# Second attention of a six-phase network on one core: its head computed in two halves, and smaller fills of the value buffers

## The chip, the cores and the metric

The kernel runs on one core of one Trainium2 chip. The metric is the time of one execution on the device, in microseconds (us). The time before is the median of three runs, 2862.56 us (2862.47 to 2865.04).

The engines are PE (matmuls; PEld is its weight load), DVE (vector), ACT (activation), POOL (GpSimd) and SP, which issues transfers. Each works off its own instructions strictly in order, and waits on semaphores for the others.

## The reference, cut to what matters

The network adds six blocks to `x` of 4 x 1024 tokens by 256: a routed feed-forward, a landmark attention, the feed-forward again, then an expert block, a quaternion attention and the expert block again. The change lies in the fifth. Its computation, for each of four groups of 1024 tokens that the kernel calls batches (in the reference, x of the whole call passes through `_layernorm`, then the attention):

```
z = layernorm(x)                       # mean and variance over 256
q = norm(quat_linear(z, qW, qb))       # four components of 64, divided by
k = norm(quat_linear(z, kW, kb))       # the root of their squares' sum
v = quat_linear(z, vW, vb)
s = q_h . k_h / 4 + constant           # 16 heads of 16
x = x + quat_linear(softmax(s) @ v, oW, ob)
```

## The kernel before, in words

Everything stays in SBUF: `X` holds all tokens as 32 tiles of 128 tokens by 256. The six phases are classes with a list of items each. An item is a tuple such as `("pj", n, b, x, h, cc)`. All five engines walk the same list and each does its own part of an item (methods `pe`, `act`, `dve`, `pool`, `sp`), with waits on semaphores whose values are counted from the list beforehand (`COUNTS`, L2827). So the order of the list is the order on every engine. If an item has a part on DVE that waits for ACT, everything behind it on DVE waits too.

**The phase `Attn1`** (L2819) works on four batches b of 8 tiles. Halves h are 4 tiles, or 512 tokens. `cc` is one of the two halves of the 256 columns; x is 0 for queries and 1 for keys. Batch 0 is prepared ahead of the loop by `start` (L2875); the other three are prepared piece by piece inside the loop of 256 turns (`order`, L2971). A turn is one key tile of one group of four heads: two pairs of score matmuls (`qk`), two exponentials of 128x1024 on ACT (L3262), and four value products (`pv`). What the head does for batch 0, and on which engine:

- `fill` (L170 to L178): matmuls of ones into an unused bank, two passes for each one asked.
- `stats` (DVE, L194, L197): mean and variance of four tiles.
- `root` (DVE, L207 to L218): twelve short instructions, each waiting for the one before, on columns of the eight tiles: the reciprocal root of the variance by a bit trick and three Newton steps. The slice of tiles comes from `rooted` (L3292), which can take a half already.
- `zz` (DVE, L3327, L222): four normalised tiles, into `ZS`. Item `(zz, n, 0, h)` is half h.
- `ht` (PE L3124, ACT L3235, DVE L3346): four transposes into a bank; ACT writes the rounded part `HB`, DVE the rest `HL`.
- `pj` (PE L162 to L164, ACT L3240; for the second query half DVE L3354): a projection of 128 columns for 512 tokens, six matmuls; the copy to `QL` adds the bias.
- `sq` (DVE L3366, L3367, L3369): the product of `QL` with itself for both column halves, and their sum; three instructions with both inputs in SBUF, the third with a wait.
- `nn` (PE L170, eight matmuls; ACT L3252, L3254): sum over the components, then the root's reciprocal by logarithm and exponential.
- `p1`, `p2`, `p3` (DVE L3389, ACT L3307, DVE L3398): `QL` times the norm, its rounded part, the rest.
- `sta` (PE L3112, then ACT L3246 or DVE L3403): these parts are placed into the rows `S` that the score matmuls read.
- `vv` (PE L162 to L164, twelve matmuls; DVE L3379): the values of two tiles, written into the value buffer.
- `put` (SP L3458): parts to a buffer in DRAM, for the later groups of heads.

**The value buffers** `V` are two tensors of 128 x 2192: 8 tiles x 16 heads x 17 columns, and 16 more. Of 17 columns, 16 are values and the last is 1, so that the value product also gives the softmax's denominator. A product reads 32 columns from a head's first one; the last head's read goes 15 beyond the 17th column, into the 16 at the end. `vone` (POOL, L3440) fills both tensors with 1.0 at the start of the phase, before the values are written into them.

**POOL's other part** is `xb` (L3446): the output bias is added to the eight tiles of `X` after both halves of `zz`, eight additions of 128x256 that read and write SBUF.

Around the head: the phase before ends with an item at which all engines meet (L3513). The first item of the head on PE is `fill` of 6, and the last is the first `qk`, which needs the keys of both halves and the queries of the first (L3112). The first batch's other items (`rest`) come in the first turns of the loop.

Of the kernel before, what the change touches and what calls it, by code (L numbers as in the profile page):

```python
# [97 lines left out]
class Chip:  # L98
# [61 lines left out]
    def mm3(self, e, o, lh, ll, rh, rl, start, stop):  # L160

        e.matmul(o, lh, rh, start=start, stop=False, skip_group_check=True)  # L162
        e.matmul(o, ll, rh, start=False, stop=False, skip_group_check=True)  # L163
        return e.matmul(o, lh, rl, start=False, stop=stop, skip_group_check=True)  # L164

    def mm_by_columns(self, e, o, l, r, start, stop):

        for j in range(4):
            js = slice(32 * j, 32 * j + 32)
            ins = e.matmul(o[js, :], l[:, js], r, start=start, stop=stop, skip_group_check=True)  # L170
        return ins
# [68 lines left out]
class Ffn0:  # L240
# [4 lines left out]

    COUNTS = {
        "up": {"up": 2, "sil": 1, "mul": 1}, "lo": {"hi": 1, "lo": 1},
        "down": {"dn": 1}, "yo": {"yo": 4, "yod": 2}, "sca": {"sca": 96}, "zput": {"zo": 16},
        "wt": {"wh": 1, "wo": 1},
        "norm": {"z": 1},  # L250
        "tp": {"ax": 1, "aa": 1, "fh": 1, "al": 1}, "lg": {"ax": 1}, "lv": {"lv": 1}, "lb": {"ax": 1, "ad": 1},
        "best": {"best": 1}, "oh": {"oh": 1}, "tot": {"ax": 1, "ad": 1}, "pos": {"ax": 1, "ad": 1, "gd": 1, "ge": 1},
        "slot": {"pm": 1},
        "oa": {"oa": 1}, "sl": {"sl": 1}, "tab": {"ad": 1, "tab": 1},
# [5 lines left out]
    def __init__(self, chip, call, first):  # L260
# [53 lines left out]
        for it in self.items:  # L314
            counts = dict(self.COUNTS.get(it[0], {}))
            if it[0] == "consts":
# [618 lines left out]
class Attn0:  # L935
# [7 lines left out]

    COUNTS = {
# [92 lines left out]
    def banks(self, p):  # L1037
# [3 lines left out]
        for it in self.items:  # L1041
            counts = dict(self.COUNTS.get(it[0], {}))
            p.count(it, counts)
# [35 lines left out]
    def pe(self, e, w, it):  # L1079
        c, p, n, k = self.c, self.c.p, self.call, it[0]  # L1080
        mm = lambda o, l, r, a=True, z=True: e.matmul(o, l, r, start=a, stop=z, skip_group_check=True)  # L1081
        if not self.COUNTS.get(k, {}).get("pp"):
            return
# [1023 lines left out]
class Ffn1:  # L2107
# [5 lines left out]
    CONSTS1 = 7, 11, 15, 19, 23, 27, 31, 39, 43, 47, 57, 60  # L2113
    COUNTS = {"b1": {"gb": 16}, "b1t": {"b1t": 1, "b1c": 1}, "io": {"io": 2, "b2z": 1}, "mh": {"wh": 1}, "mk": {"wo": 1}, "b2": {"b2l": 32, "b2": 1},
# [704 lines left out]
class Attn1:  # L2819
# [5 lines left out]

    ahead = ()
    PARTS = ((0, 1, 0), (0, 0, 1))  # L2827
    COUNTS = {"root": {"rt": 1}, "vone": {"vone": 2}, "zz": {"zb": 1}, "xb": {"xb": 8},
# [46 lines left out]
    def start(self):  # L2875

        n = self.call
        seq = []
        hts = lambda h: [("ht", n, 0, h, cc) for cc in range(2)]
        parts = lambda x, h: [(k, n, 0, x, 0, h) for k in ("p1", "p2", "p3")]  # L2880
        pj = lambda x, h, cc: ("pj", n, 0, x, h, cc)
        seq.append(("fill", n, 6))
        seq += [("stats", n, "p", 0, 0), ("stats", n, "p", 0, 4), ("root", n, "p", 0), ("zz", n, 0, 0), ("zz", n, 0, 1)]
        seq += hts(0) + hts(1) + [pj(1, 0, 0), pj(1, 0, 1), ("sq", n, 0, 1, 0)]
        seq += [pj(1, 1, 0), pj(1, 1, 1), ("nn", n, 0, 1, 0), ("sq", n, 0, 1, 1), pj(0, 0, 0)] + parts(1, 0)
        seq += [pj(0, 0, 1), ("sq", n, 0, 0, 0), ("nn", n, 0, 1, 1), ("vv", n, 0, 0)] + parts(1, 1)
        seq += [("nn", n, 0, 0, 0)] + [("sta", n, 1, jj, h) for h in range(2) for jj in range(2)] + [("put", n, 1)]
        seq += parts(0, 0) + [("fill", n, 3)] + [("sta", n, 0, jj, 0) for jj in range(2)]
        rest = Jobs()
        rest.add(0, pj(0, 1, 0))  # L2890
        rest.add(1, pj(0, 1, 1), ("sq", n, 0, 0, 1))
        rest.add(1, ("vv", n, 0, 1))
        rest.add(1, ("nn", n, 0, 0, 1), *parts(0, 1))
        rest.add(1, ("vv", n, 0, 2))
        rest.add(1, ("sta", n, 0, 0, 1))
        rest.add(1, ("sta", n, 0, 1, 1), ("put", n, 0), ("stk", n, 1))
        rest.add(1, ("vv", n, 0, 3), ("xb", n, 0))
        for x in range(2):
            for k in ("p1", "p2", "p3"):
                rest.add(1, (k, n, 0, x, 1))  # L2900
        return seq, rest
# [413 lines left out]
    def dve(self, e, w, it):  # L3315
        c, p, n, k = self.c, self.c.p, self.call, it[0]
# [10 lines left out]
        elif k == "zz":  # L3327
            b, h = it[2:]
            if b:
                w.wait_ge(*p.at("pp", ("nn", n, b - 1, 1, 1) if b > 1 else ("nn", n, 0, 0, 1)))  # L3330
            w.wait_ge(*p.at("rt", ("root", n, "p", b)))
            for i in range(4 * h, 4 * h + 4):
                ins = c.normalise(e, self.ZB[:, i, :], 8 * b + i)
            ins.then_inc(*p.one("zb"))
        elif k == "ht":
            b, h, cc = it[2:]
# [11 lines left out]
        elif k == "pj" and self.by(it) == "fv":  # L3348
            b, x, h, cc = it[2:]
# [6 lines left out]
        elif k == "sq":  # L3356
            b, x, h = it[2:]
# [6 lines left out]
            pj = ("pj", n, b, x, h, 1)  # L3364
# [5 lines left out]
        elif k == "vv":  # L3370
            b, i2 = it[2:]
# [11 lines left out]
        elif k == "p1":  # L3383
            b, x, cc = it[2:5]
            h, hs = it[5] if len(it) > 5 else 1, self.span(it)
# [6 lines left out]
        elif k == "p3":  # L3392
            b, x, cc = it[2:5]
# [5 lines left out]
        elif k == "sta" and self.by(it) == "fv":  # L3399
            x, jj, h = it[2:]  # L3400
# [9 lines left out]
        elif k == "ft":  # L3410
            u = it[2]
            b, g, hf = self.half(8 * u)
# [9 lines left out]
        elif k == "fb":  # L3422
            b, h, cc = it[2:]
# [3 lines left out]
        elif k == "fo":  # L3427
            b, i2 = it[2:]
# [6 lines left out]
    def pool(self, e, w, it):  # L3435
        c, p, n, k = self.c, self.c.p, self.call, it[0]
        if k == "vone":
            for v in self.V:
                w.wait_ge(*p.mine())
                e.memset(v[:, :], 1.0).then_inc(*p.one("vone"))  # L3440
        elif k == "xb":
            b = it[2]
            w.wait_ge(*p.at("zb", ("zz", n, b, 1)))
            for i in range(8 * b, 8 * b + 8):
                w.wait_ge(*p.mine())
                e.tensor_tensor(c.X[:, i, :], c.X[:, i, :], self.k.BVO[:, 1, :], ALU.add).then_inc(*p.one("xb"))  # L3446
# [233 lines left out]
```

## Time and profile before

| | |
|---|---|
| median of three runs | 2862.56 us |
| the profiled execution's own time | 2869.36 us |
| its span | 2867.6 us |
| PE busy | 2766.3 us, 96% |
| DVE busy | 1834.8 us, 64% |
| ACT busy | 1633.8 us, 57% |
| POOL busy | 551.3 us, 19% |
| mean granted TensorE clock | 0.990 |

The profile is of one execution. Its times count from the first instruction, and the execution's own time is 1.8 us longer than the span. Busy time is the sum of an engine's instructions. A timeline row gives the start, the duration, the engine, the line of the kernel, what is written from what, and in brackets how long the engine stood idle before it and what it then waited for. The granted clock is a share of 2.4 GHz. Merged rows (x4, x8) give the time from the first start to the last end.

### The profile page before, as it was taken

Reading aid. Unit: us, or ns where it says so; the run is one execution under the profiler, and the core shown is the slowest. Engines: PE = TensorE matmul, PEld = TensorE weight load, DVE = VectorE, ACT = ScalarE, POOL = GpSimd, SP = SyncE. Lnnn points to the kernel's source line nnn. Section 1 sums busy time; section 2 is a strip of 40 time slices with the busy share of each in tenths; the row PEclk is TensorE's granted clock in tenths of the full one; section 3 lists DMA queues with packets and bytes.
Section 4 is the critical chain, followed back from the end, with each engine's and each line's share of the span. In section 5 each row is a group of like instructions: output and inputs, shape, how many; then the busy total and the mean of one; then the engine's idle time right before and its main releaser. Section 6 shows DMA issues by size and latency. Waiting matters only on the chain.

```text
span 2867.6 us, 56389 instructions
## 1 busy us (share of the span) xinstructions
PE 2766.3 (96%) x23301; PEld 2160.6 (75%) x23301; DVE 1834.8 (64%) x3730; ACT 1633.8 (57%) x2473; POOL 551.3 (19%) x479
## 2 busy tenths in 40 slices
PE   9999999998999999999999988998999999998998
PEld 7888999996777778889999965996343434333998
DVE  8775555548887787755555567887545464436786
ACT  4434454543443455344554433776887888892786
POOL 0002224221000000021323146553000000001454
PEclk9999999999999999999999999999999999999999
DMA  5123333332000022233433253774452252513686
GB/s 169 63 67 115 95 88 84 86 92 70 2 3 24 3 71 82 67 98 87 102 77 93 77 160 119 212 212 118 100 133 52 70 116 80 113 38 119 181 215 149
DMA packets 237312, 279.77 MB, mean 98 GB/s; under 512 B 23267, under 2 KB 218496, under 8 KB 237056
## 3 DMA queue, kind: packets, MB, share of 16 engines
q1 hardware_dynamic: 204992, 229.78, 27.3%
q0 software_dynamic: 30720, 45.85, 8.5%
q8 instruction: 184, 3.01, 0.5%
q10 hardware_dynamic: 1344, 0.53, 0.1%
q14 instruction: 72, 0.59, 0.1%
HBM read 204.58 MB, written 72.88 MB: 97 GB/s over the span
## 4 chain that ended last, share of the span: by engine, by line
PE 78%; DVE 11%; ACT 4%; issue 3%; POOL 2%; DMA 1%; POOLq 0%; DVEq 0%; ACTq 0%
PE PS L162 18%; PE PS L164 17%; PE PS L163 17%; PE PS L3112 13%; PE PS L1081 6%; PE PS L170 2%; POOL ZR L222 1%; DVE SM L194 1%; ACT FW L581 1%; DVE SM L1461 1%; ACT Z L626 1%; PE PS L515 1%; DVE FW L666 1%; PE PS L3205 1%; DVE PROD L654 1%
## 5 line engine op out<-in xcount | busy, mean ns | idle before, releaser
L3262 ACT ACTIVATE P<-PS 128x1024 f32<-128x1024 f32 x512 | 484.5, 1045 | 85.3 <-PE PS L3112 83.4
L162 PE MATMUL PS<-FH,FW 128*128 128x366 f32 (+1 forms) x1408 | 504.5, 358 | 9.3 <-ACT SIL L559 4.7
L164 PE MATMUL PS<-FH,FW 128*128 128x366 f32 (+1 forms) x1408 | 497.7, 353 | 0.0
L163 PE MATMUL PS<-FH,FW 128*128 128x366 f32 (+1 forms) x1408 | 496.9, 353 | 0.0
L567 ACT ACTIVATE FHH<-PROD 128x366 fp32r<-128x366 f32 (+1 forms) x352 | 194.3, 552 | 421.3 <-DVE PROD L654 394.3
L162 PE MATMUL PS<-FW,FHH 128*122 128x256 f32 (+1 forms) x1184 | 338.5, 286 | 1.5 <-DVE FHH L661 1.5
L163 PE MATMUL PS<-FW,FHH 128*122 128x256 f32 (+1 forms) x1184 | 332.4, 281 | 0.0
L164 PE MATMUL PS<-FW,FHH 128*122 128x256 f32 (+1 forms) x1184 | 332.0, 280 | 0.0
L654 DVE TENSOR_TENSOR PROD<-SIL,PS 128x366 f32<-128x366 f32 (+1 forms) x352 | 206.6, 587 | 157.6 <-PE PS L164 137.2
L661 DVE TENSOR_TENSOR FHH<-PROD,FHH 128x366 fp32r<-128x366 f32 (+1 forms) x352 | 208.9, 594 | 147.3 <-ACT FHH L567 145.2
L162 PEld LDWEIGHTS PS<-FH,FW 128*128 128x128 f32 x1408 | 265.5, 189 | 35.4 <-ACT SIL L559 8.4
L164 PEld LDWEIGHTS PS<-FH,FW 128*128 128x128 f32 x1408 | 265.2, 188 | 22.5
L163 PEld LDWEIGHTS PS<-FH,FW 128*128 128x128 f32 x1408 | 265.5, 189 | 19.0 <-issue 1.0
L3112 PE MATMUL PS<-P,V 128*32 128x512 f32 x2048 | 273.4, 606 | 1.3 <-DVE OC L3409 0.3
L666 DVE TENSOR_TENSOR FW<-WST,FW 128x1536 fp32r<-128x1536 f32 x96 | 168.7, 1757 | 138.4 <-ACT FW L581 131.4
L559 ACT ACTIVATE SIL<-PS 128x366 f32<-128x366 f32 (+1 forms) x352 | 180.7, 513 | 124.3 <-PE PS L164 119.5
L879 POOL DMA_INDIRECT xa_scratch<-Z,RV x84 | 139.7, 1664 | 533.5 <-ACT Z L626 481.1
L162 PEld LDWEIGHTS PS<-FW,FHH 128*122 128x122 f32 (+1 forms) x1184 | 219.6, 185 | 5.6 <-DVE FHH L661 2.3
L163 PEld LDWEIGHTS PS<-FW,FHH 128*122 128x122 f32 (+1 forms) x1184 | 219.6, 185 | 2.3
L164 PEld LDWEIGHTS PS<-FW,FHH 128*122 128x122 f32 (+1 forms) x1184 | 219.6, 185 | 0.0
L869 POOL DMA_INDIRECT Z<-zn_scratch,RV x84 | 96.0, 1143 | 515.5 <-DVE RV L843 429.0
L3112 PE MATMUL PS<-S,S 64*128 64x512 f32 x1024 | 193.0, 451 | 1.6 <-DVE S L3403 1.0
(485 smaller groups left out, 5557.0 us busy)
## 6 DMA issues: line engine op xcount, KB each, us to landing
WS<-L_ffn_w_dram SPq DMA_DIRECT2D x256, 256.0 KB
WST<-L_ffn_W_dram SPq DMA_DIRECT2D x168, 256.0 KB
S<-parts_scratch SPq DMA_DIRECT2D x60, 384.0 KB, 7.6
parts_scratch<-PT SPq DMA_DIRECT2D x28, 512.0 KB, 3.8
WST<-L_ffn_W1s_dram SPq DMA_DIRECT2D x40, 256.0 KB
WST<-L_ffn_W3s_dram SPq DMA_DIRECT2D x40, 256.0 KB
WST<-L_ffn_W2s_dram SPq DMA_DIRECT2D x40, 256.0 KB
xa_scratch<-X SPq DMA_DIRECT2D x17, 512.0 KB, 5.1
```

The costliest lines, as they stand in the source:

```text
L162: e.matmul(o, lh, rh, start=start, stop=False, skip_group_check=True)
L163: e.matmul(o, ll, rh, start=False, stop=False, skip_group_check=True)
L164: return e.matmul(o, lh, rl, start=False, stop=stop, skip_group_check=True)
L559: e.activation(self.SIL[:, h, 0:NH], c.bank(2 * self.up_at[it] % 3, NH), ACT.Silu).then_inc(*p.one("sil"))
L567: e.activation(self.FHH[:, s % 2, 0, hs], self.PROD[:, h, 0:NH], ACT.Copy).then_inc(*p.one("hi"))
L654: e.tensor_tensor(self.PROD[:, h, 0:NH], self.SIL[:, h, 0:NH], c.bank((2 * self.up_at[it] + 1) % 3, NH), ALU.mult).then_inc(*p.one("mul"))
L661: e.tensor_tensor(self.FHH[:, s % 2, 1, hs], self.PROD[:, h, 0:NH], self.FHH[:, s % 2, 0, hs].bitcast(F32), ALU.subtract).then_inc(*p.one( ...
L666: e.tensor_tensor(self.fw(q)[:, 1, :], self.WST[:, q % 2, :], self.fw(q)[:, 0, :].bitcast(F32), ALU.subtract).then_inc(*p.one("wo"))
L879: e.indirect_dma_start(out=c.XA, out_offset=bass.IndirectOffsetOnAxis(ap=self.TO.bitcast(U32)[:, 6 * e_ + t:6 * e_ + t + 1], axis=0), in_= ...
L1081: mm = lambda o, l, r, a=True, z=True: e.matmul(o, l, r, start=a, stop=z, skip_group_check=True)
L3112: mm = lambda o, l, r, a=True, z=True: e.matmul(o, l, r, start=a, stop=z, skip_group_check=True)
L3262: e.activation(self.PR[K % 3][:, 2 * jj:2 * jj + 2, :].rearrange("p a b -> p (a b)"), c.pair(2 * ((2 * K + jj) % 3)), ACT.Exp, scale=0.25) ...
```

## The change

The list of the head is rewritten for halves. The root is now two items of four tiles, and `zz` of the first half follows its root directly; the statistics of the second half, its root and its rows come later. One `fill` is added, and the order of the projections, squares, norms and parts differs. Each `zz` of batch 0 waits for its own root. POOL fills only every 17th column and the last 16 of each value buffer, in four instructions in place of two.

```diff
-    COUNTS = {"root": {"rt": 1}, "vone": {"vone": 2}, ...
+    COUNTS = {"root": {"rt": 1}, "vone": {"vone": 4}, ...
...
         seq.append(("fill", n, 6))
-        seq += [("stats", n, "p", 0, 0), ("stats", n, "p", 0, 4), ("root", n, "p", 0), ("zz", n, 0, 0), ("zz", n, 0, 1)]
-        seq += hts(0) + hts(1) + [pj(1, 0, 0), pj(1, 0, 1), ("sq", n, 0, 1, 0)]
-        seq += [pj(1, 1, 0), pj(1, 1, 1), ("nn", n, 0, 1, 0), ("sq", n, 0, 1, 1), pj(0, 0, 0)] + parts(1, 0)
-        seq += [pj(0, 0, 1), ("sq", n, 0, 0, 0), ("nn", n, 0, 1, 1), ("vv", n, 0, 0)] + parts(1, 1)
+        seq += [("stats", n, "p", 0, 0), ("root", n, "p", 0, 0), ("zz", n, 0, 0), ("stats", n, "p", 0, 4)]
+        seq += hts(0) + [("fill", n, 1), ("root", n, "p", 0, 1), ("zz", n, 0, 1)]
+        seq += [pj(1, 0, 0), pj(1, 0, 1), ("sq", n, 0, 1, 0)] + hts(1) + [pj(0, 0, 0), ("nn", n, 0, 1, 0), pj(0, 0, 1)]
+        seq += [pj(1, 1, 0), pj(1, 1, 1)] + parts(1, 0)
+        seq += [("sq", n, 0, 1, 1), ("sq", n, 0, 0, 0), ("nn", n, 0, 1, 1), ("vv", n, 0, 0)] + parts(1, 1)
         seq += [("nn", n, 0, 0, 0)] + [("sta", n, 1, jj, h) for h in range(2) for jj in range(2)] + [("put", n, 1)]
...
-            w.wait_ge(*p.at("rt", ("root", n, "p", b)))
+            w.wait_ge(*p.at("rt", ("root", n, "p", b) if b else ("root", n, "p", b, h)))
...
             for v in self.V:
                 w.wait_ge(*p.mine())
-                e.memset(v[:, :], 1.0).then_inc(*p.one("vone"))
+                e.memset(v[:, 16:2176:17], 1.0).then_inc(*p.one("vone"))
+                w.wait_ge(*p.mine())
+                e.memset(v[:, 2176:2192], 1.0).then_inc(*p.one("vone"))
```

## Rows read from the trace of the kernel before

**Rows 1.** The page, part 4: the chain that ended last, by engine.
```profile
PE 78%; DVE 11%; ACT 4%; issue 3%; POOL 2%; DMA 1%; POOLq 0%; DVEq 0%; ACTq 0%
```

**Rows 2.** Timeline of PE: start, us, line, out<-in, idle before and releaser.
```profile
1250.72 0.79 PE L162 MATMUL PS<-FH,FW 128*128 128x512 f32 x1 [2.78 <-issue]
...
1973.07 5.42 PE L178 MATMUL PS<-ONES 128*128 128x512 f32 x12 [0.83 <-DVEq L3513]
1982.09 3.67 PE L3124 MATMUL PS<-IDENT,ZS 128*128 128x128 f32 x16 [3.60 <-DVE ZS L222]
...
1988.10 0.40 PE L162 MATMUL PS<-HB,WHk 128*128 128x512 f32 x1
...
1989.47 0.39 PE L162 MATMUL PS<-HB,WHk 128*128 128x512 f32 x1
...
1992.66 1.06 PE L170 MATMUL PS<-ONT,SQM 128*32 128x512 f32 x8 [0.30 <-DVE ONT L3369]
1993.65 0.50 PE L162 MATMUL PS<-HB,WHq 128*128 128x512 f32 x1
...
1997.59 0.39 PE L162 MATMUL PS<-WHv,HB 128*128 128x256 f32 x1
...
2007.62 0.73 PE L3112 MATMUL PS<-S,S 64*128 64x512 f32 x4 [1.04 <-DVE S L3403]
...
2046.91 0.66 PE L3124 MATMUL PS<-IDENT,ZS 128*128 128x128 f32 x4
2047.49 0.73 PE L3112 MATMUL PS<-S,S 64*128 64x512 f32 x4
```

**Rows 3.** Stretches: us, busy PE, PEld, DVE, ACT, POOL (instructions), PEclk, DMA, GB/s.
```profile
1250.00:1254.00 4.00, 3.28 (x9) 2.70 (x10) 0.36 (x1) 0.60 (x1) 1.60 (x2) 0.57 0.75 233
...
1982.00:1985.70 3.70, 3.61 (x17) 3.38 (x17) 2.77 (x8) 1.79 (x3) 2.13 (x3) 0.50 1.09 362
```

**Rows 4.** Timeline of DVE: statistics, first root step and rows of the head.
```profile
1973.10 1.41 DVE L194 BATCH_NORM_STATS2 SM<-X 128x6 f32<-128x256 f32 x4
...
1976.81 1.59 DVE L207 TENSOR_SCALAR SM<-SM 128x8 f32<-128x8 f32 x1
...
1980.65 2.67 DVE L222 TENSOR_SCALAR ZS<-X,SM 128x256 f32<-128x256 f32 x8
```

**Rows 5.** Timeline of DVE: first and last of the next root's twelve instructions.
```profile
2025.71 0.17 DVE L207 TENSOR_SCALAR SM<-SM 128x8 f32<-128x8 f32 x1
...
2027.94 0.17 DVE L218 SCALAR_TENSOR_TENSOR SM<-SM 128x8 f32<-128x8 f32 x1
```

**Rows 6.** Timeline of POOL in the head.
```profile
1972.91 1.55 POOL L2556 DMA_INDIRECT xa_scratch<-YE,SM  x1 [0.30 <-issue]
1973.89 4.49 POOL L3440 MEMSET V<- 128x2192 f32 x2
1983.41 6.40 POOL L3446 TENSOR_TENSOR X<-X,BVO 128x256 f32<-128x256 f32 x8 [5.03 <-DVE ZS L222]
```

**Rows 7.** POOL's groups by form: a short fill; busy us, mean ns, idle before.
```profile
L2744 POOL MEMSET SQM<- 128x128 f32 x1 | 0.2, 204 | 0.1
```

**Rows 8.** Timeline of DVE: the first squares, and a subtraction behind ACT's rounding.
```profile
1990.49 0.69 DVE L3366 TENSOR_TENSOR ONT<-QL 128x512 f32<-128x512 f32 x1 [3.30 <-ACT QL L3240]
...
1996.59 0.69 DVE L3398 TENSOR_TENSOR QLR<-QL,PT 128x512 fp32r<-128x512 f32 x1 [0.72 <-ACT PT L3307]
```

**Rows 9.** Timeline of ACT: a projection's copy, and the rounding of a part.
```profile
1989.67 0.69 ACT L3240 ACTIVATE QL<-PS,C 128x512 f32<-128x512 f32 x1 [0.68 <-PE PS L164]
...
1995.93 0.62 ACT L3307 ACTIVATE PT<-QL 128x512 fp32r<-128x512 f32 x1
```

**Rows 10.** Timeline of all engines near 1753: DVE's products beside POOL's.
```profile
1751.23 2.71 POOL L2770 TENSOR_TENSOR Wk<-WLk,C 64x256 f32<-64x256 f32 x4
...
1753.26 0.21 DVE L2494 TENSOR_TENSOR PX<-PX 128x64 f32<-128x64 f32 x1
1753.51 0.52 DVE L2496 TENSOR_TENSOR PX<-PX 128x64 f32<-128x64 f32 x1
```

More of the change, by code:

```diff
@@ L2827 @@
     PARTS = ((0, 1, 0), (0, 0, 1))
-    COUNTS = {"root": {"rt": 1}, "vone": {"vone": 2}, "zz": {"zb": 1}, "xb": {"xb": 8},
+    COUNTS = {"root": {"rt": 1}, "vone": {"vone": 4}, "zz": {"zb": 1}, "xb": {"xb": 8},
               "ht": {"pp": 1, "fv": 1}, "eb": {"eb": 1}, "sta": {"pp": 1}, "sq": {"sqv": 1}, "p1": {"prv": 1}, "qk": {"qkp": 1, "ex": 1},
```

## The prediction

> **What bounds the kernel now.** I began with the page's chain of waits: 78% of what ended last is PE, 11% DVE, 4% ACT [rows 1]. So time moves where PE stands still, and the diff touches one such place, the head of the second attention. I then read the timelines of the engines from 1973 us, where the expert phase has ended, to the first score matmul at 2007.62 [rows 2]. From there on the list is untouched and PE nearly back to back; so **the change is worth what it does to that 2007.62**, and I expect the shift to reach the end whole.
>
> Inside the head PE isn't the limit. It waits 3.60 us for DVE's rows before the transposes [rows 2], and those run at a granted clock of 0.50, the 1.2 GHz level [rows 3]. DVE first takes the statistics of four tiles twice, 1.86 us each (half of 1973.10 to 1976.81). Then the root's first step takes 1.59 us [rows 4], where the same step of the next root takes 0.17 [rows 5]. It ends at 1978.40; POOL's fills of the value buffers end at 1973.89 + 4.49 = 1978.38 [rows 6]. I read that as DVE shut out by POOL.
>
> **The change, step by step.** It halves the root and the rows, takes the fills nearly away, and reorders the list. I rebuilt the schedule from durations of before; a time below is on that execution's axis.
>
> 1. *Fills.* A fill of 128x128 takes 0.20 us [rows 7]; four fills of 128 or 16 columns with their gaps are under 1 us, but they start only when the indirect transfer leaves POOL (1972.91 + 1.55) [rows 6], so they end near 1975.3. The root now starts at 1974.96. Bounds of its wait: 0 and 0.35 us; I take 0.2. Some 1.2 us of the 1.42 us stall are gone.
> 2. *First half.* A root is twelve steps; without the stall it takes 2.42 us (2025.71 to 2028.1) [rows 5]. The steps are 8 columns wide, so I charge four tiles the same. 1974.96 + 0.2 + 2.42 = 1977.58. Four rows of the eight that take 2.67 are 1.33 [rows 4], and PE is let go 1.44 after they start (1980.65 to 1982.09) [rows 2, 4]: transposes at **1979.02**, 3.07 earlier. At full clock four transposes take 0.58 (2046.91 to 2047.49) [rows 2]: both groups are done at 1980.20, the new fill (two passes of 0.45, where 12 take 5.42) at 1981.10 [rows 2]. DVE is in the second statistics until 1978.91 + 1.86 = 1980.77, then makes two subtractions of a 128x512 tile, 0.69 each at most [rows 8], and PE starts its projections at 1982.25. A projection of six matmuls is 1.37 (1988.10 to 1989.47) [rows 2]: two end at 1984.98.
> 3. *Second half.* The second root is 2.42 us of DVE that was not there: 1982.05 to 1984.47. Rows until 1985.80, transposes 1985.91 to 1987.09, a query projection to 1988.45. ACT copies the second projection 0.2 after its end (1989.47, 1989.67) and DVE squares 0.74 later [rows 2, 9]: 1985.92. Before it was 1990.49 [rows 8], so here the change is 4.57 ahead.
> 4. *A collision that was not there.* POOL's eight additions of the output bias (6.40 in all, 0.73 and a gap each) wait for the second rows. Before, they ran 1983.41 to 1989.81 [rows 6], and DVE's first product with both inputs in SBUF came at 1990.49 [rows 8]. Now they start at 1985.91, on top of the squares. What an overlap costs is seen at 1753: while POOL multiplies out of SBUF, a DVE product of 128x64 takes 0.52 instead of 0.21; the one of 0.21 stands right behind another [rows 10]. The squares are three instructions, the second right behind the first, the third behind a wait of its own: I charge two waits of one POOL addition, 1.45. Bounds 0 and 2.2 (three waits). The squares let PE go 2.17 after their start (1990.49 to 1992.66) [rows 2, 8]: 1985.92 + 2.17 + 1.45 = 1989.54. The norm sum takes 0.99 (1992.66 to 1993.65) [rows 2], then come a query projection and both of the keys' second half, 3 x 1.37: PE is through at **1994.63**. Without the collision at 1993.5.
> 5. *The order behind it.* The list puts the three parts of the keys' first half behind both late key projections and ahead of the late squares. ACT's rounding copy so queues behind ACT's copies of those projections: the last one 1994.83 to 1995.43 (a pass of ACT over 128x512 takes 0.62) [rows 9]. DVE's subtraction comes 0.66 after the rounding starts (1995.93, 1996.59) [rows 8, 9], at 1996.09, and the squares queued behind it at 1996.72. PE's next item is the norm sum of these: 1996.72 + 2.17 = **1998.89; PE stands 4.26 us**.
> 6. *The end of the head.* Norm sum 0.99, then the value projection: 1999.88 against 1997.59 [rows 2], 2.29 late. From there to 2007.62 every step is the same in the same order: **+2.3 us** at full clock.
> 7. *The clock.* Behind PE's idle of 3.60 us the stretch 1982 to 1985.7 has 0.50, behind one of 2.78 (at 1250.72) the stretch 1250 to 1254 has 0.57 [rows 2, 3]. Behind 4.26 I expect it again. Norm sum and value projection then cost up to their length once more, 1.0 and 1.3 (of 0.99 and 1.5): **+2.3**. Bounds 0 and 3.5 (the fill behind them too, if its slack is gone). PE's full clock at the front is in the times above.
>
> SP's transfers keep their places and are late by the same amount; nothing before 2028 waits for one.
>
> **Sum:** +1.2 (the order and the second root, all gains counted), +1.1 (the collision: what PE's slack leaves of 1.45), +2.3 (clock) = +4.6. The profiled execution took 2869.36 (span 2867.6 and 1.8 around it), 6.8 above the median of 2862.56; with the sum it is 2874.0, and on the median **2867.2**. A measurement can tell 0.2%, 5.7 us, from no change; this lies inside.
>
> *A rule weighed.* The rows at 1753 show a neighbour that paid nothing [rows 10]. The Trainium skill, page "SBUF — State Buffer", section "Who interferes with whom", says that a DVE instruction with two SBUF inputs and a GpSimd instruction that reads SBUF exclude each other, the second to issue waiting out the whole first. Taken at its word for each of the three instructions, the squares pay 2.2.
>
> **Rivals.**
> - *One of the two prices is missing.* Collision without the low clock: +2.3, 2864.9. Low clock without collision: +3.6, 2866.2. For it: PE worked for long ahead of the gap. Chance 0.22.
> - *Neither*: +1.2, 2863.8. Chance 0.08.
> - *Three waits in the squares*, POOL slipping in between each two: +0.7 more, 2867.9; against it stands the free neighbour. Chance 0.08. The page's rule would give this.
> - *Slower*: PE's clock falls in the middle too. Between 1981.1 and 1989.5 PE idles 1.15, 0.9 and 1.1 us. If the level is low from about 1987, the projections behind cost up to 1.2 more each (DVE hides a part), and the tail is low again: +6.2, 2868.8. It decides from an idle near 2.8 us, the shortest that has a low stretch behind it in my rows; two more us of delay in the squares would make one. Chance 0.12.
> - *Faster*: PE has its last first-half work done 2 us earlier than before; if the rounding did not hold the late squares, the tail would start early: -1.5, 2861.0. Against it: each engine takes the list strictly in order. Chance 0.10.
> - *It doesn't do what it says*: the strided fills still hold the root, for 1 us: +0.8 on top of any case; inside the range.
>
> **Numbers.** The forecast has 0.40. All cases but the slower one lie in 2861 to 2868; with the unknowns of the clock and a spread of 2.6 us between the runs I take 2860.5 to 2870.5. Slower by over 0.2% (above 2868.3): most of the slower rival and the upper part of the forecast, 0.20. Faster by as much needs -5.7: 0.02. Same: 0.78.
>
> **What would show it.** The first root step under 0.5 us; transposes near 1979; the first squares stretched beside POOL's additions; an idle of PE near 4 us ahead of the norm sum of the keys' second half, with a clock near 0.5 behind; the first score matmul 36.8 to 39.1 us after the first statistics (before: 2007.62 - 1973.10 = 34.52). I am wrong if that distance is under 34.5, if PE has no idle over 2 us there, or if the loop swallows the shift.

## The result, and the profile after

The changed kernel takes 2866.69 us in the median of 21 runs (2863.47 to 2871.78), the kernel before 2862.94 beside it (21 runs, 2860.28 to 2865.25). The ratio is 1.0015, with a 95% interval of 1.0009 to 1.0021: slower by some 4 us. That is inside the 0.2% that I had called "same", on the side and of about the size that was forecast (+4.6).

In one profiled execution of each, the head grows by more than the medians differ. Let D be the time from the first statistics to the first score matmul: 34.52 us before, 2007.63 - 1967.36 = **40.27** after. Everything after it keeps its length in this pair: from the first score matmul to the end of the span 859.98 us before, 859.37 after. Over the fourteen profiled executions shown below that stretch lies between 855.9 and 860.0, and for the kernel before it is 3.5 shorter in its second profile than in its first. So a total follows D only loosely; here the interval of the ratio, +2.6 to +6.0 us, holds both the 3.75 of the medians and the 5.75 of D. (The head starts at 1967.36 here and at 1973.10 before; over the executions shown below this start moved between 1967.4 and 1977.8, and the change can't reach what lies ahead of it. So times below are compared from the first statistics on.)

The timeline of DVE of the changed kernel; the first rows answer to [rows 4], the squares to [rows 8]:

```profile
1967.36 1.41 DVE L194 BATCH_NORM_STATS2 SM<-X 128x6 f32<-128x256 f32 x4
...
1969.21 0.36 DVE L207 TENSOR_SCALAR SM<-SM 128x4 f32<-128x4 f32 x1
...
1971.86 1.38 DVE L222 TENSOR_SCALAR ZS<-X,SM 128x256 f32<-128x256 f32 x4
...
1980.90 1.16 DVE L3367 TENSOR_TENSOR ONT<-QL 128x512 f32<-128x512 f32 x1 [0.21 <-ACT QL L3241]
1981.98 1.23 DVE L3368 TENSOR_TENSOR N<-QL 128x512 f32<-128x512 f32 x1
1983.24 1.10 DVE L3370 TENSOR_TENSOR ONT<-ONT,N 128x512 f32<-128x512 f32 x1
...
1991.13 0.69 DVE L3399 TENSOR_TENSOR QLR<-QL,PT 128x512 fp32r<-128x512 f32 x1 [3.21 <-ACT PT L3308]
```

The root's first step is down from 1.59 to 0.36 us: the fills have let go. But the squares of the keys' first half, 0.69 each where nothing stands beside them, take 1.16, 1.23 and 1.10. And DVE stands 3.21 us for ACT's rounding before it may begin the late squares. POOL, answering to [rows 6]:

```profile
1969.52 0.91 POOL L3441 MEMSET V<- 128x128 f32 x1
1970.48 0.11 POOL L3443 MEMSET V<- 128x16 f32 x1
...
1980.78 7.75 POOL L3449 TENSOR_TENSOR X<-X,BVO 128x256 f32<-128x256 f32 x8 [9.64 <-DVE ZS L222]
```

The eight additions now begin just ahead of the squares and take 7.75 us for 6.40: both sides pay. PE, answering to [rows 2]:

```profile
1967.33 7.10 PE L178 MATMUL PS<-ONES 128*128 128x512 f32 x12 [0.83 <-DVEq L3516]
1974.27 1.04 PE L3125 MATMUL PS<-IDENT,ZS 128*128 128x128 f32 x8
...
1984.48 1.06 PE L170 MATMUL PS<-ONT,SQM 128*32 128x512 f32 x8 [1.25 <-DVE ONT L3370]
...
1993.81 1.16 PE L170 MATMUL PS<-ONT,SQM 128*32 128x512 f32 x8 [3.95 <-DVE ONT L3370]
...
1997.76 1.19 PE L170 MATMUL PS<-ONT,SQM 128*32 128x512 f32 x8
...
2001.35 4.54 PE L178 MATMUL PS<-ONES 128*128 128x512 f32 x6
2005.82 0.50 PE L3113 MATMUL PS<-PT,EB 32*128 32x512 f32 x2
...
2007.63 0.73 PE L3113 MATMUL PS<-S,S 64*128 64x512 f32 x4 [1.07 <-DVE S L3404]
```

The transposes come 6.91 us after the first statistics (before 8.99), so the halves and the small fills did what they are for. Then the lead is lost. The norm sum of the late keys comes 26.45 after the statistics, behind 3.95 us of idle; before it came at 23.50. From it to the next norm sum are 3.95 us (with a high clock 2.61, below), and the last fill takes 4.54 us where six such passes take 2.84. The granted clock in stretches, answering to [rows 3]:

```profile
1967.40:1970.00 2.60, 2.60 (x3) 1.10 (x4) 2.46 (x11) 2.53 (x5) 2.29 (x3) 0.50 0.44 50
...
1995.00:1998.00 3.00, 3.00 (x16) 2.73 (x20) 0.82 (x2) 1.32 (x2) 0.00 (x0) 0.50 0.01 3
1998.50:2001.00 2.50, 1.42 (x15) 0.63 (x8) 1.80 (x4) 1.78 (x4) 0.00 (x0) 1.00 0.00 0
2001.50:2004.50 3.00, 3.00 (x4) 1.27 (x5) 2.00 (x3) 1.34 (x3) 0.00 (x0) 0.50 0.94 197
```

The clock falls three times. One fall is behind the idle of 3.95 us, as expected. Two are unexpected: one at the head's first matmul, and one under the last fill, after the clock had been back at 1.00 and PE had idled only 1.08 us.

### The profile page after: what moved, and what is told of

It reads as the page before. It is cut to its first block, busy times and chain, and to the rows that moved or that the text cites. A ratio compares the mean times of both kernels' runs of the same rounds, so it can differ in the third digit from the quotient of the medians.

```text
span 2867.0 us, 56407 instructions
## 1 busy us (share of the span) xinstructions
PE 2766.8 (97%) x23303; PEld 2158.9 (75%) x23303; DVE 1836.7 (64%) x3742; ACT 1632.9 (57%) x2473; POOL 549.7 (19%) x481
## 4 chain that ended last, share of the span: by engine, by line
PE 78%; DVE 11%; ACT 4%; issue 3%; POOL 2%; DMA 2%; SPq 0%; POOLq 0%; DVEq 0%; ACTq 0%
PE PS L162 18%; PE PS L164 17%; PE PS L163 17%; PE PS L3113 13%; PE PS L1081 6%; PE PS L170 2%; POOL ZR L222 1%; DVE SM L194 1%; ACT FW L581 1%; DVE SM L1461 1%; ACT Z L626 1%; PE PS L178 1%; PE PS L515 1%; DVE FW L666 1%; PE PS L3206 1%
## 5 line engine op out<-in xcount | busy, mean ns | idle before, releaser
L162 PEld LDWEIGHTS PS<-FH,FW 128*128 128x128 f32 x1408 | 265.2, 188 | 31.3 <-ACT SIL L559 8.4
L3113 PE MATMUL PS<-P,V 128*32 128x512 f32 x2048 | 273.3, 606 | 1.3 <-DVE OC L3410 0.5
L3113 PE MATMUL PS<-S,S 64*128 64x512 f32 x1024 | 193.0, 451 | 1.6 <-DVE S L3404 1.1
```

## The experiments

A difference of 1 us in 2863 is below what five rounds tell (their intervals are 5 to 6 us wide). So each run has its ratio, and the reading rests on D and on the rows of its profiled execution. "Low start" says that the clock was at 0.50 in the first us of the head, where the lists don't differ yet. D has one blind spot: in two of these executions (parts_early, old_small_fills_warm) the clock was at 0.50 for some 3.4 us just behind the first score matmul, which D doesn't count.

| kernel | D, us | start | ratio to before, 95% interval |
|---|---|---|---|
| before (first profile) | 34.52 | high | |
| before_again | 34.02 | high | 0.9998 (0.9989 to 1.0007) |
| changed kernel | 40.27 | low | 1.0015 (1.0009 to 1.0021) |
| same_again | 40.34 | low | 1.0013 (1.0004 to 1.0021) |
| bias_later | 37.49 | high | 1.0012 (1.0003 to 1.0021) |
| gap_filled | 36.90 | high | 1.0010 (1.0001 to 1.0018) |
| parts_early | 37.18 | high | 1.0011 (1.0002 to 1.0020) |
| three_mended | 35.87 | high | 1.0004 (0.9995 to 1.0013) |
| new_big_fills | 44.40 | low | 1.0030 (1.0019 to 1.0041) |
| old_small_fills | 32.33 | high | 0.9992 (0.9983 to 1.0001) |
| old_small_fills_warm | 32.07 | high | 0.9994 (0.9985 to 1.0003) |
| old_warm_bias_later | 31.40 | high | 0.9993 (0.9984 to 1.0002) |
| best | 29.85 | high | 0.9991 (0.9982 to 1.0000) |
| best_again | 29.86 | high | 0.9985 (0.9976 to 0.9994) |

**The changed kernel again.**

> The changed kernel unchanged, to see what varies. Let D be the time from the first statistics of the head to the first score matmul: 34.52 us in the profile of before, 40.27 in that of after, though the medians differ by 3.75 only. Theory: in the profiled execution of after TensorE's clock was already low when the head began (0.50 and 0.57 from 1968 to 1971), which held the first transposes up by some 1.0 us; without that D would be 39.2. I expect D of 38.2 to 40.3, and a total of before + 3.7. Rival (the loss in the profile is the real one and the medians hide a part): D 40.3 again and + 5.7.

D is 40.34, and the low start is there again, so the theory's 38.2 to 40.3 is missed by a hair and the run can't separate the two. What separates them are the next three runs, whose lists are the same up to the transposes and whose start is high: their transposes come 5.79, 5.86 and 5.99 us after the statistics against 6.91 and 6.88 here. A low start costs the changed list 0.9 to 1.1 us at that point, 0.7 at the first squares (13.5 against 12.8), and 0.5 at the late norm sum (26.45 against 25.91 in the run with the gap filled, whose list is the same up to the idle before that sum).

**POOL's additions later.**

```diff
             w.wait_ge(*p.at("zb", ("zz", n, b, 1)))
+            if b == 0:
+                w.wait_ge(*p.at("qkp", ("qk", n, 12, 1)))
             for i in range(8 * b, 8 * b + 8):
```

> POOL's eight additions for the first batch wait for the thirteenth turn's scores, so that none runs beside the head. Collision theory: the three squares of the keys' first half, 1.16 + 1.23 + 1.10 us in the profile of after, go back to 0.69 each; from their start to the norm sum on TensorE 2.17 instead of 3.58; the late projections and all behind them come 1.1 to 1.4 us earlier, total some 1.2 under the changed kernel, so before + 2.5. Rival (the squares are slow for another reason, such as the activation engine writing the same banks): no change in them, before + 3.7.

The timelines of DVE and PE of this run:

```profile
1977.77 1.41 DVE L194 BATCH_NORM_STATS2 SM<-X 128x6 f32<-128x256 f32 x4
...
1990.52 0.69 DVE L3367 TENSOR_TENSOR ONT<-QL 128x512 f32<-128x512 f32 x1 [0.19 <-ACT QL L3241]
1991.13 0.68 DVE L3368 TENSOR_TENSOR N<-QL 128x512 f32<-128x512 f32 x1
1991.85 0.69 DVE L3370 TENSOR_TENSOR ONT<-ONT,N 128x512 f32<-128x512 f32 x1
```
```profile
1992.80 1.06 PE L170 MATMUL PS<-ONT,SQM 128*32 128x512 f32 x8
...
2002.16 1.93 PE L170 MATMUL PS<-ONT,SQM 128*32 128x512 f32 x8 [3.95 <-DVE ONT L3370]
...
2006.89 1.53 PE L170 MATMUL PS<-ONT,SQM 128*32 128x512 f32 x8
...
2010.48 2.84 PE L178 MATMUL PS<-ONES 128*128 128x512 f32 x6
```

The squares are back to 0.69. From the first statistics to the late norm sum it is 2002.16 - 1977.77 = 24.39, against 25.91 in the next run, which has the collision and the same high start: 1.52 us. The collision is shown and its price as well. PE's idle of 3.95 us is untouched, and there is a low clock behind it (norm sum 1.93 for 1.06). But it falls once only: from one norm sum to the next it is 4.73 us, and the last fill has its 2.84 us again. The total, +3.4 us by the ratio with an interval from 0.9 to 6.0, can't tell the two theories (+2.5 and +3.7) apart.

**PE's gap filled.**

```diff
-... ("sq", n, 0, 0, 0), ("nn", n, 0, 1, 1), ("vv", n, 0, 0)] + parts(1, 1)
+... ("sq", n, 0, 0, 0), ("fill", n, 4), ("nn", n, 0, 1, 1), ("vv", n, 0, 0)] + parts(1, 1)
```

> A fill of eight passes of ones (3.6 us) stands in TensorE's idle time ahead of the norm sum of the keys' second half. Clock theory: the granted clock stays at 1.00 from there to the first scores; the value projection takes 1.5 us instead of 2.7, the fill ahead of the last placements 2.7 instead of 4.5 and no longer delays them; D shorter by 1.2 + 1.5 = 2.7, total before + 1.0. Rival (the tail hangs on the vector engine alone, the slow matmuls lie in its shadow): total before + 3.7 within 0.5.

PE and the clock from the filled gap on:

```profile
1995.97 3.60 PE L178 MATMUL PS<-ONES 128*128 128x512 f32 x8
2000.09 1.06 PE L170 MATMUL PS<-ONT,SQM 128*32 128x512 f32 x8 [0.52 <-DVE ONT L3370]
...
2002.70 1.07 PE L170 MATMUL PS<-ONT,SQM 128*32 128x512 f32 x8
...
2005.63 0.50 PE L3113 MATMUL PS<-PT,EB 32*128 32x512 f32 x2 [1.20 <-DVE QLR L3399]
...
2006.30 2.84 PE L178 MATMUL PS<-ONES 128*128 128x512 f32 x6
2009.30 0.50 PE L3113 MATMUL PS<-PT,EB 32*128 32x512 f32 x2 [0.16 <-DVE QLR L3399]
```
```profile
1999.00:2002.00 3.00, 2.48 (x17) 1.08 (x16) 2.90 (x5) 0.75 (x2) 0.00 (x0) 1.00 0.00 0
2002.00:2006.00 4.00, 2.80 (x23) 1.35 (x21) 2.50 (x4) 2.41 (x5) 0.00 (x0) 1.00 0.01 2
```

The clock stays at 1.00, and PE stood idle 1.20 us ahead of the placements before the last fill (the first row of L3113). From one norm sum to the next it is 2.61 us (changed kernel 3.95), and from the second to the last placements 6.60 (changed kernel 2005.82 - 1997.76 = 8.06). So the two falls of the clock cost the changed kernel 1.34 + 1.46 = 2.8 us of D. The last placements now wait for DVE; in the changed kernel they waited for the slow fill ahead of them. The total didn't follow as far: +2.8 us by the ratio, with an interval of 0.3 to 5.2, where I had said +1.0. D itself is 2.4 over the first profile of before and 2.9 over the second.

**The keys' parts earlier.**

```diff
-        seq += [pj(1, 1, 0), pj(1, 1, 1)] + parts(1, 0)
+        seq += parts(1, 0) + [pj(1, 1, 0), pj(1, 1, 1)]
```

> The three parts of the keys' first half are put ahead of the two late key projections in the list, so that the activation engine's rounding isn't queued behind the copies of those. Order theory: the subtraction leaves the vector engine before the late squares are due, these start 0.6 to 1.2 us earlier, with TensorE's idle shorter by as much; total before + 2.5 to + 3.1. Rival (the rounding never held anything, the late squares wait for the late projection): before + 3.7, squares at the same distance from the last projection (2.3 us after its last matmul starts).

ACT, and PE's late norm sum, in this run:

```profile
1994.50 0.63 ACT L3308 ACTIVATE PT<-QL 128x512 fp32r<-128x512 f32 x1
1995.11 0.69 ACT L3241 ACTIVATE QL<-PS,C 128x512 f32<-128x512 f32 x1
1996.47 0.69 ACT L3241 ACTIVATE QL<-PS,C 128x512 f32<-128x512 f32 x1 [0.67 <-PE PS L164]
```
```profile
1999.26 1.74 PE L170 MATMUL PS<-ONT,SQM 128*32 128x512 f32 x8 [2.83 <-DVE ONT L3370]
```

The rounding runs ahead of the two copies, and the late norm sum is at 1999.26 - 1974.63 = 24.63 against 25.91: 1.28 us, and PE's idle is down from 3.95 to 2.83. The order theory holds, a little above the 0.6 to 1.2 that it said. The clock was still low behind 2.83 us (norm sum 1.74; 4.17 us from there to the next), and once only up to the first score: the last fill took 2.84.

**All three mended.** The wait for the additions, the parts early, and `("fill", n, 2)` in what is left of the gap.

> The changed kernel with the three repairs at once: additions later, the keys' parts ahead of the late projections, a fill of four passes in what is left of the gap. If collision (1.5 us), order (1.3) and clock (2.8 with a high clock at the head's start) are all of it and add up, D is 36.9 - 1.5 - 1.2 = 34.2 with a high clock at the start and 34.8 to 35.2 with a low one, so the level of before (34.52), and the total before + 0 within 1. Rival (one of the three only moved the wait elsewhere): D 35.5 or more.

D is 35.87. By the number that is the rival's case (35.5 or more), but not by its reason. The late norm sum comes after 23.43 us, which is 25.91 - 1.52 - 1.28 = 23.11 and 0.3 more, so two of the three add up. The last fill was slow again, under a clock that had been at 1.00 until the placements ahead of it (PE had idled 1.20 us for a subtraction):

```profile
2000.62 0.50 PE L3113 MATMUL PS<-PT,EB 32*128 32x512 f32 x2 [1.20 <-DVE QLR L3399]
...
2001.47 4.28 PE L178 MATMUL PS<-ONES 128*128 128x512 f32 x6
```
```profile
2001.00:2003.00 2.00, 2.00 (x6) 0.84 (x3) 1.48 (x3) 1.24 (x3) 0.00 (x0) 0.50 0.67 139
```

With a fill of 2.84 this D would be 34.4, an estimate from the 9.81 us between the second norm sum and the first score, which are 8.38 where that fill is quick. So mending all three brings the halves back to about the level of before (34.52 and 34.02), not ahead of it; that holds with the slow fill counted out, and no run has shown it.

**Each part of the change alone.** First the fills, in the list of before (`vone` as in the changed kernel):

> Only the second part of the change: the list of before with the small fills of the value buffers. Port theory: the first step of the root takes 0.17 us instead of 1.59, rows and transposes come 1.42 us earlier. With the clock low as before, D is 33.7 to 33.1 and the total before - 0.8 to - 1.4; if TensorE's idle ahead of the transposes, 2.2 us instead of 3.6, leaves the clock high, D is 31.4 and the total before - 3.2. Rival (the root's first step is slow for a reason of its own): no change.

```profile
1971.45 1.41 DVE L194 BATCH_NORM_STATS2 SM<-X 128x6 f32<-128x256 f32 x4
...
1975.16 0.17 DVE L207 TENSOR_SCALAR SM<-SM 128x8 f32<-128x8 f32 x1
...
1977.58 2.67 DVE L222 TENSOR_SCALAR ZS<-X,SM 128x256 f32<-128x256 f32 x8
```

The rows come 6.13 us after the statistics; before it was 1980.65 - 1973.10 = 7.55: the 1.42 us of the stall, exactly. D is 32.33, below the 33.1 to 33.7 that I expected with a low clock: 2.2 under the first profile of before, 1.7 under the second. The second is the fair neighbour, since its low stretch at the transposes is as short as here (some 3.4 us, in the first profile some 6.8), and there the root's first step took 1.88, a stall of 1.71. So the fills are worth just the stall that they take away, and in the head they were a gain by themselves; for the total it isn't shown, as the interval of the ratio, 0.9983 to 1.0001, holds 1.

Then the list, with the buffers filled whole:

> Only the first part: the new list with the whole value buffers filled as before. Port theory: the first root of four tiles starts 1.85 us after the first statistics and then stands until the second fill ends, some 3.4 us later (before 1974.96 against 1978.38): D longer than in the changed kernel by 2.5 to 3.3, total before + 6.3 to + 7. Rival (fills and root don't meet): as the changed kernel, before + 3.7.

```profile
1969.61 1.72 DVE L207 TENSOR_SCALAR SM<-SM 128x4 f32<-128x4 f32 x1
...
1975.32 1.38 DVE L222 TENSOR_SCALAR ZS<-X,SM 128x256 f32<-128x256 f32 x4
```

From the root's first step to the rows it is 5.71 us, for 2.65 in the changed kernel (1969.21 to 1971.86). The root's first two steps take 1.72 and 1.94 us, for 0.36 and 0.25: the second has to wait too. D is 4.1 longer than there, more than the 2.5 to 3.3 that I expected, and the total is 8.6 over before by the ratio (8.0 by the medians). The 3.1 us of the rows are what the theory said; the rest came with a clock that was low for some 7 us, from 1.2 us behind the first transposes on. This list cannot do without the small fills: its earlier root meets nearly the whole of POOL's work.

**Towards a better version.** The list of before with the small fills and `("fill", n, 8)`:

> The list of before with the small fills, and eight fills asked in place of six, so that TensorE works almost until the transposes are ready. Theory: clock 1.00 at the transposes (0.58 for four instead of 0.92) and in the first projection (1.37 instead of 2.34); D 31.3 to 31.6, total before - 3.0. Rival (the head is bound by the vector engine from the first squares on, the faster front only makes it wait): before - 1.4.

The clock is 1.00 throughout the head, but D is 32.07, only 0.26 better, and misses the 31.3 to 31.6. The first squares came 14.23 us after the statistics, for 15.20, and so the first two ran into POOL's additions, which in the run before were ending as they began:

```profile
1985.67 0.85 DVE L3366 TENSOR_TENSOR ONT<-QL 128x512 f32<-128x512 f32 x1 [2.69 <-ACT QL L3240]
1986.44 1.23 DVE L3367 TENSOR_TENSOR N<-QL 128x512 f32<-128x512 f32 x1
```

With the additions later as well:

> The list of before, small fills, eight fills asked, and POOL's additions for the first batch behind the thirteenth turn. In the run with the same list but the additions in place D was 32.07 and the first two squares took 0.85 and 1.23 us. Collision theory: they take 0.69, and D is 31.1 to 31.5; total before - 3.1. Rival (nothing gained, the additions end before they matter): D 32.1.

D is 31.40 and the squares are 0.69: as expected, and the 0.67 that D gains are the 0.70 that the two squares had lost. The last step fills the 0.7 us that DVE spends on each rounding:

```diff
-        seq += [pj(0, 0, 1), ("sq", n, 0, 0, 0), ("nn", n, 0, 1, 1), ("vv", n, 0, 0)] + parts(1, 1)
-        seq += [("nn", n, 0, 0, 0)] + [("sta", n, 1, jj, h) for h in range(2) for jj in range(2)] + [("put", n, 1)]
-        seq += parts(0, 0) + [("fill", n, 3)] + ...
+        seq += [pj(0, 0, 1), ("sq", n, 0, 0, 0), ("nn", n, 0, 1, 1), *parts(1, 1)[:2], ("vv", n, 0, 0), parts(1, 1)[2]]
+        seq += [("nn", n, 0, 0, 0)] + [("sta", n, 1, jj, 0) for jj in range(2)] + parts(0, 0)[:2]
+        seq += [("sta", n, 1, jj, 1) for jj in range(2)] + [parts(0, 0)[2], ("put", n, 1), ("fill", n, 2)] + ...
```

> A version meant to beat both. The list of before with small fills, eight fills, additions later; and the 0.7 us that the vector engine waits for each rounding are filled: the value copy goes between the rounding and the subtraction of the keys' second half, and the first queries' product and rounding go ahead of the keys' last placements. Worked out from the durations of before: D 29.7 against 31.3 without the last two, total before - 4.8. Rival (the rounding isn't what the tail waits for): D as in the run with the unchanged tail, before - 3.

The tail of the head on DVE in this version:

```profile
1993.20 0.68 DVE L3379 TENSOR_TENSOR V<-PS,BVO 128x512 f32<-128x512 f32 x1
1993.98 0.69 DVE L3398 TENSOR_TENSOR QLR<-QL,PT 128x512 fp32r<-128x512 f32 x1
1994.63 0.75 DVE L3403 TENSOR_SCALAR S<-PS,C 128x512 fp32r<-128x512 f32 x1
1995.33 0.69 DVE L3389 TENSOR_TENSOR QL<-QL,N 128x512 f32<-128x512 f32 x1
1995.94 0.75 DVE L3403 TENSOR_SCALAR S<-PS,C 128x512 fp32r<-128x512 f32 x1
```

No row has an idle in brackets: other work lies between each product and its subtraction. D is 29.85, for 29.7 worked out. The total, 2.6 us under before by the ratio (3.9 by the medians), is short of the 4.8 expected; D, and not the total, rules out the rival (D as in the run with the unchanged tail).

**Controls.** The kernel before and the best version, each once more.

> The kernel before, unchanged, for two things: what the comparison gives where nothing differs (ratio 1.0000 within 0.0008), and how much D moves in a list where TensorE idles 3.6 us ahead of the transposes. Theory: a low clock at the head's start lies in that idle time, so D stays at 34.5 within 0.3 whichever level the first fill meets. Rival: D 1 us or more longer with a low start.

> The best version a second time, on this chip beside the kernel before: total before - 2.5 to - 4.7, D 29.85 with a high clock at the start, and up to 1.5 us more with a low one, since its first fills end just as the transposes are due.

The comparison of the kernel before with itself gives 0.9998. Its D was 34.02, with a high start, so the question of a low start in this list stays untested; the 0.5 us come from a shorter low stretch at the transposes, 0.2 more than I had allowed. The best version has D 29.86 and a total of 2858.82 us (11 runs) against 2862.81: ratio 0.9985, 0.9976 to 0.9994. **It beats both kernels**: the one before by 4 us (1.7 to 6.9), which is clear of noise though below 0.2% of the time, and, worked out over the kernel before, the changed one by some 8 us.

## Why the prediction was right

The time moved as forecast: +4.6 said, 3.75 measured in the medians. The order of reasons holds too, with two terms sized in the wrong place. That 4.6 and 3.75 lie so close is in part luck: in the profiled execution D grew by 5.75, and two profiles of the same kernel differ by 0.5 in D and by 3.5 behind it.

- *Fills (step 1).* 0.2 us of waiting said; the first step took 0.36 for 0.17, the second 0.25, so 0.27 in all, and 0.12 and 0.18 in two other runs of this list. Right, and the rival of the strided fills that hold the root for 1 us falls.
- *First half (step 2).* Transposes at 5.92 us after the statistics said; 5.79 to 5.99 in the three runs with a high start. Right.
- *Second half (step 3).* Squares at 12.82 said; 12.75 to 12.95 in those runs. Right. One row was misread by a hair: from ACT's copy to the squares it is 0.82 us (1989.67 to 1990.49), not 0.74.
- *Collision (step 4).* 1.45 us said, in two waits of 0.73; measured from the squares' start to the norm sum 3.58 for 2.17, so 1.41. The sum is right and its split is wrong: all three instructions pay, 0.41 to 0.54 each. The free neighbour from which I took two waits [rows 10] did not carry over. The Trainium skill (page "SBUF — State Buffer", section "Who interferes with whom") has a DVE instruction with two SBUF inputs contend with a GpSimd instruction that reads SBUF, so it lets all three pay, and the trace agrees with it here. The 2.2 us at which I priced that, a whole addition each time, are too much. An addition may be partly over when the DVE instruction comes, but the first had run only 0.12 us (1980.78 to 1980.90) and cost 0.47, so why the price is lower is not shown.
- *Order (step 5).* Norm sum of the late keys at 25.79 said; 25.91 with a high start. Idle 4.26 said, 3.95 measured. I had given ACT's copy 0.62 us, which is the row of the rounding; the copy's own takes 0.69.
- *End of the head (step 6).* +2.3 us with a high clock said; D of the run with the gap filled is 36.90, +2.4 against the first profile of before, +2.9 against the second. Right within that.
- *Clock (step 7).* +2.3 us said: 1.0 at the norm sum, 1.3 at the value projection, none at the fill. In two runs where the clock was low from the late norm sum on (bias_later, new_big_fills) that is what came: 4.73 and 4.72 us to the next norm sum for 2.61, 2.1 in all, and a fill of 2.84. The changed kernel's two profiles have another course. The first fall came when the norm sum was nearly through (1.16 for 1.06) and cost 1.34; then the clock was back, and fell a second time under the fill, which cost 1.46. So 2.8 were measured, in two falls where I had priced one. "The fill has slack" was the assumption that failed: of the 1.70 us by which it grew, 1.46 reached D. The upper bound of 3.5 had named it, the value taken had not. And an idle near 2.8 us is not the shortest with a low stretch behind it, as I had read from my rows: here it was one of 1.08 us.
- *What I left out*: the low start, 1.1 us at the transposes and 0.5 left at the late norm sum, in an execution that has it. It was not in the profile of before.

By these terms D after would be 34.52 + 2.4 + 2.8 + 0.5 = 40.2, and 40.27 was measured. The medians differ by 3.75 only. The profiles show one execution each, and how often a low start or a slow last fill comes in the others isn't to be seen from totals. Nor does their spread tell: the runs of the changed kernel lie within 8.3 us, those of before within 5.0 beside them, but within 4.5 to 8.5 in four later comparisons.

The rivals: the price of the collision and that of the clock are both there, so "one of the two missing" and "neither" fall for the profiled execution. "Three waits in the squares" has its three waits, but at 1.41 us and not at 2.2. "Slower" (a fall in the middle) did not come: the clock was 1.00 from 1971 to 1994.5. "Faster" falls, since DVE did stand 3.21 us for the rounding. The forecast's distance from first statistics to first score, 36.8 to 39.1, was missed in the profile by 1.2 (40.27).

## What to carry to other kernels

If an item is issued earlier, ask what else was released by the same event: here eight additions on another engine started with the second rows and ran beside work they had never met. In a list worked off in order, a short instruction that is queued behind another engine's later work can eat up what the reordering advanced (here DVE stood 3.21 us for one rounding); look at each engine's own order, not at the item's place in the whole. And look at what PE does behind a gap: in all five profiles of this list where PE stood idle for 2.8 us or more ahead of the late norm sum, a low clock followed, and in the two with a fill in that gap the norm sums kept their 1.07 us. In the one with the gap filled but for 0.52 us that gave 2.8 us of D back.

## What the runs showed of the hardware

- The same past, two clocks. In 14 profiled executions PE's work over the 12 us ahead of the head has the same waits within 0.01 us (0.60, 0.88, 0.83 us), and in three of them the granted clock fell to 0.50 at the head's first matmul. It stayed at 1.00 in eleven. The three are among the seven profiles of the list in halves (the changed kernel, same_again, new_big_fills), and none among the seven of the list of before and its versions; whether that is chance the runs don't tell. A stretch of 2.7 us from there on, in same_again and then in parts_early, whose lists are the same up to that point:

```profile
1972.30:1975.00 2.70, 2.70 (x4) 1.15 (x5) 2.53 (x12) 2.62 (x6) 2.15 (x5) 0.50 0.76 82
```
```profile
1974.60:1977.30 2.70, 2.70 (x7) 1.26 (x8) 2.49 (x12) 2.62 (x6) 2.28 (x5) 1.00 0.50 51
```

- The same short idle, two clocks. Ahead of the placements before the last fill PE idled 1.08, 1.15 and 1.20 us in the changed kernel, same_again and three_mended, and the clock fell behind it, as that fill began. It idled 1.20 us at the same place in gap_filled and parts_early, and the fill ran at 1.00.
- POOL's fill of an SBUF tensor holds up even a DVE instruction of 8 columns: the root's first step took 1.59 and 1.88 us for 0.17 in two profiles of the kernel before. The statistics of the second four tiles, just ahead of it and beside the same fills (1974.96 to 1976.37, fills 1973.89 to 1978.38), took the 1.41 us that they take without them.
